# Bias and mask of a second attention enter its scores on TensorE instead of VectorE

## The chip, the cores and the metric

One Trainium2 chip, one of its cores. The metric is the device time of one execution of the whole kernel in microseconds, the median of three runs.

## What is computed

A two-layer decoder block over 128 sequences of 64 positions with 128 features, all in float32: causal attention, a gated cross layer, a mixture of experts, then a second layer with causal attention, cross-attention with a bias, and a second mixture of experts. The change is in the cross-attention of the second layer (16 heads of 8, `attn_bias` and `attention_mask` the same for all heads of a sequence):

```python
qh = (q @ Wq + bq).reshape(b, n, HEADS, DK).transpose(0, 2, 1, 3)
kh = (k @ Wk + bk).reshape(b, -1, HEADS, DK).transpose(0, 2, 1, 3)
vh = (v @ Wv + bv).reshape(b, -1, HEADS, DK).transpose(0, 2, 1, 3)
scores = jnp.einsum('bhnd,bhmd->bhnm', qh * scale, kh)
scores = scores + attn_bias[:, None, :, :] + attention_mask[:, None, :, :]
probs = jax.nn.softmax(scores, axis=-1)
ctx = jnp.einsum('bhnm,bhmd->bhnd', probs, vh)
```

## The kernel before

The 8192 rows (128 sequences x 64 positions) are cut into 64 tiles of 128 rows; a tile holds two whole sequences. The kernel runs in stages, one after the other over all tiles: the first layer's attention, a table of position products, a third stage (the first layer's gated cross layer and the attention of its expert block), the first experts, the fifth stage (from 2790 to about 3810 us), the second experts, a last sum.

The fifth stage combines the first experts' output into x4 (`combine5`, VectorE L1837 to L1842, from rows that GpSimd fetches at L2084), normalises it (L1537), runs the causal attention (called `a5[0]`, "the first attention"), a layer norm, the cross-attention (`a5[1]`, "the second attention"), another norm, and the logits of the router. It is one software pipeline. Each engine has a hand-written `period(i, j)` that lists its work for several tiles at once: in period i the causal attention is at tile i, the cross-attention's scores at tile i-2, its output at tile i-3, x4 at tile i+2. An engine executes its list strictly in this order; between engines there are counting semaphores, and `after(engine, signals...)` makes an engine wait for given counts. The loop over periods is unrolled four times.

TensorE's list of one period: weighted sum of the second attention (`weigh5`, L907); output projection of the first (L1054); transposition of x4 for tile i+2 (L1066, waits for `norms[0]`, that is, for VectorE's L1537); scores of the second attention for tile i-2 (`scores5`, L892); two transpositions (L1072, L1075); turning of the first attention's probabilities (`turn5`, L901); queries and keys of tile i+2 (L1084); router logits and keys (L1089, L1093); weighted sum of the first attention (L907); projection (L1054); values (L921); half of the turning of the second attention's probabilities; masks (L881) and scores (L892) of the first attention for tile i+1; the other half; then x5's transposition (L1115) and query (L1120).

`scores5` writes 128 rows x 16 heads x 64 keys into two PSUM banks of 512 columns, by four products of a 64x64 quarter of the array each, with the keys of the head pairs spread into a block-diagonal form (GpSimd's `spread5`, L1989, twice a period: b_k into `shared`, rope_k into `k_bd`). For the causal attention, a bf16 product of the identity with the mask starts the banks (`masks`, L881) and the scores are added to it. The second attention's scores start the banks themselves. GpSimd has added bias and mask of the tile once, 128x64, into `fm` (L2092). VectorE then adds `fm` to the scores, broadcast over 8 heads, one bank at a time (`bias_and_shift5`: add L1828, max L1831, subtract L1833), with the norm's L1537 between the two banks. For the first attention `shift5` (max L1551, subtract L1553) reads the PSUM bank directly. ScalarE takes the exponential (L1256) and copies turned probabilities (L1260). VectorE's list of a period goes on with `divide5` of the first attention (L1543, L1545), rope (L1559), the sum and norm statistics of tile i-3, `combine5` and statistics for tile i+3, and the shift of the first attention's scores for tile i+1; the next period begins with L1537 for x4.

Of the kernel before, what the change touches and what calls it, by code (L numbers as in the profile page):

```python
# [29 lines left out]
ALU = mybir.AluOpType  # L30
AX = mybir.AxisListType.X

P = 128
S = 64
# [6 lines left out]
NR = 2  # L41
V = 4
U = 2
# [57 lines left out]
def build(nc, T, out):  # L101
    B = T["x"].shape[0]
    NT = B * S // P
# [4 lines left out]
    with ExitStack() as ctx:  # L108
# [29 lines left out]
        scores_ps = ps("scores_ps", [P, U, NR, 512])  # L138
# [213 lines left out]
        def attention(a, tiles, shift_start, shift_per):  # L352

            return Attention(Signal(sc_ready[a], tiles), Signal(sub_ready[a], shift_start, shift_per), Signal(exp_ready[a], 2 * tiles, 2),
                             Signal(tr_ready[a], 2 * tiles, 2), Signal(tr_copied[a], 2 * tiles, 2), Signal(pv_ready[a], tiles),
                             Signal(ctx_ready[a], 2 * tiles, 2), Signal(ct_ready[a], tiles))
# [33 lines left out]
        norm_rstd = [again(m_rstd), again(f_rstd), again(r4_added)]  # L390
        rotated, rope_added, a_spread, b_spread = again(f_rotated), again(f_added, 2), again(m_spread), again(f_spread)
        fm_added, x5b_added = again(g_spread), again(xb_added)
        a5 = [attention(0, NT, 4 * NT, 4), attention(1, 2 * NT, 8 * NT, 6)]

        hop_dram = dram("hop_dram", [B * S, MH * S])
        xn_dram, r4_dram = dram("xn_dram", [B * S, D]), dram("r4_dram", [B * S, D])
# [327 lines left out]
        def _(pe):  # L724
# [152 lines left out]
            pe.wait_ge(s["hop_out0"], S + CREDIT)  # L877
            pe.wait_ge(s["hop_out1"], S + CREDIT)

            def masks(a, bank):  # L880
                pe.matmul(bank, ident16, causal16.unsqueeze(1).broadcast_to([P, 8, S]), start=True, stop=False,  # L881
                          skip_group_check=True)

            def scores5(at, a, q, keys, causal):
                if causal:
                    for g in range(NR):
                        masks(a, scores_ps[:, a, g, :])
                by_pair = keys.rearrange("p (h t) -> p h t", t=P)
                for g in range(NR):
                    rows = slice(64 * g, 64 * g + 64)  # L890
                    for b in range(NB):
                        last = pe.matmul(scores_ps[S * b:S * b + S, a, g, :], q[rows, S * b:S * b + S],  # L892
                                         by_pair[rows, :, S * b:S * b + S], start=not causal, stop=True,
                                         skip_group_check=True)
                last.then_inc(at.score.sem, 1)

# [30 lines left out]
            def period(i, j):  # L927
# [61 lines left out]
                    pe.matmul(desk_ps[:, 0:8], x_T[u], f_gate[:], start=True, stop=True, skip_group_check=True)\  # L989
                      .then_inc(f_logits.sem, 1)  # L990
                if live(i - 1):
                    after(pe, f_spread.of(i - 1), a3.copied.of(i - 2))
                    scores5(a3, 1, q_ring[:, 1 - u, :], k_ring[2 + 1 - u], True)
                if live(i + 1):
                    after(pe, m_copied.of(i + 1), m_v_ready.of(i + 1), gated.of(i + 7), block_done.of(i + 5) if j4 == 2 else gated.of(i + 7),
                          mixed.of(i, 5))
# [60 lines left out]
            def period(i, j):  # L1057
# [7 lines left out]
                    after(pe, norms[0].of(i + 2), rotated.of(i + 1))  # L1065
                    pe.transpose(heads_ps[:, 0:P], x4[(j + 2) % UN], ident).then_inc(x4_turned.sem, 1)  # L1066
                if live(i - 2):
                    after(pe, (zeroed, U + 1), b_q_copied.of(i - 2), b_spread.of(i - 2), a5[1].copied.of(i - 3))
                    scores5(a5[1], 1, b_q[u], k_ring[2 + u], False)
                if live(i - 4):  # L1070
                    after(pe, norms[2].of(i - 4), a_v_copied.of(i + 1), b_q_copied.of(i - 2), logits_copied.of(i - 5))
                    pe.transpose(desk_ps[:, 0:P], x6[u], ident).then_inc(x6_turned.sem, 1)  # L1072
# [33 lines left out]
                if live(i - 2):  # L1106
                    turn5(a5[1], 1, i - 2, 0)
                if live(i + 1):
                    after(pe, a_spread.of(i + 1), a5[0].copied.of(i))
                    scores5(a5[0], 0, q_ring[:, 1 - u, :], k_ring[1 - u], True)  # L1110
                if live(i - 2):
                    turn5(a5[1], 1, i - 2, 1)
                if live(i - 1):
# [310 lines left out]
        def _(dve):  # L1424
# [397 lines left out]
                dve.tensor_copy(got_w[u], weight[:, :, bass.ds(tile, 1)].rearrange("p k t -> p (k t)"))\  # L1822
                   .then_inc(s["weights_got"], 1)

            def bias_and_shift5(n, u, g):
                biased = probs[1][:, 512 * g:512 * g + 512].rearrange("p (h t) -> p h t", t=S)
                best = row_max[1][:, 8 * g:8 * g + 8]
                dve.tensor_tensor(biased, scores_ps[:, 1, g, :].rearrange("p (h t) -> p h t", t=S),  # L1828
                                  fm[u].unsqueeze(1).broadcast_to([P, 8, S]), ALU.add).then_inc(a5[1].shift.sem, 1)
                after(dve, a5[1].shift.of(n, 3 * g + 1))  # L1830
                dve.tensor_reduce(best, biased, AX, ALU.max).then_inc(a5[1].shift.sem, 1)  # L1831
                after(dve, a5[1].shift.of(n, 3 * g + 2))
                dve.tensor_tensor(biased, biased, best.unsqueeze(2).broadcast_to([P, 8, S]), ALU.subtract)\  # L1833
                   .then_inc(a5[1].shift.sem, 1)

            def combine5(n, u):
                dve.tensor_copy(got_w[u], weight[:, :, bass.ds(n, 1)].rearrange("p k t -> p (k t)")).then_inc(norms[0].sem, 1)  # L1837
                after(dve, norms[0].of(n, 1), (in_loaded[u], X4_LOADS + 8 * (n - u) + 16), (got_loaded[u], 16 * (n - u) + 32))
# [6 lines left out]
            def period(i, j):  # L1845
                u = j % U
                if live(i + 2):
                    apply5(norms[0], 0, u, x4[(j + 2) % UN], x4_raw[u], norm_rstd[0].of(i + 2), x4_turned.of(i - 2))
                if live(i - 4):
                    apply5(norms[2], 2, u, x6[u], b_sum[u], norm_rstd[2].of(i - 4), (x6_stored[u], 8 * (i - 4 - u) + 16), x6_turned.of(i - 6))  # L1850
                if live(i - 3):
                    divide5(a5[1], 1, i - 3)
                if live(i - 1):
                    after(dve, out_ready[0].of(i - 1))
                    dve.tensor_tensor(a_sum[1 - u], heads_of[0][:, 256:384], x4[(j - 1) % UN], ALU.add).then_inc(norms[1].sem, 1)
                    stats5(norms[1], 1, 1, i - 1, 1 - u, a_sum[1 - u])
                if live(i - 2):
                    after(dve, a5[1].score.of(i - 2), fm_added.of(i - 2))
                    bias_and_shift5(i - 2, u, 0)
                if live(i - 1):  # L1860
                    apply5(norms[1], 1, 1 - u, x5[1 - u], a_sum[1 - u], norm_rstd[1].of(i - 1), x5_turned.of(i - 3), x5b_added.of(i - 3))
                if live(i - 2):
                    bias_and_shift5(i - 2, u, 1)
                if live(i):
                    divide5(a5[0], 0, i)
                if live(i + 2):
                    after(dve, a_roped.of(i + 2), rope_added.of(i))
                    rope5(rotated, u)
                if live(i - 3):
                    after(dve, out_ready[1].of(i - 3), x5b_added.of(i - 3))  # L1870
                    dve.tensor_tensor(b_sum[1 - u], heads_of[1][:, 256:384], x5b[(j - 3) % UN], ALU.add).then_inc(norms[2].sem, 1)
                    stats5(norms[2], 1, 2, i - 3, 1 - u, b_sum[1 - u])
                if live(i + 3):
                    combine5(i + 3, 1 - u)
                    stats5(norms[0], 3, 0, i + 3, 1 - u, x4_raw[1 - u])
                if live(i + 1):
                    after(dve, a5[0].score.of(i + 1))
                    shift5(a5[0], 0, i + 1, 0)
                    shift5(a5[0], 0, i + 1, 1)
# [58 lines left out]
        def _(pool):  # L1938
# [149 lines left out]
            def period(i, j):  # L2088
                u = j % U
                if live(i - 1):  # L2090
                    after(pool, (c_loaded[1 - u], SIDE_LOADS + 24 * (i - 1 - (1 - u)) + 48), a5[1].shift.of(i - 3))
                    pool.tensor_tensor(fm[1 - u], fm_in[1 - u][:, 0:S], fm_in[1 - u][:, S:2 * S], ALU.add)\  # L2092
                        .then_inc(fm_added.sem, 1)
                    after(pool, norms[1].of(i - 1, norms[1].per - 1))
                    rstd5(norm_rstd[1], 1, 1 - u)
# [80 lines left out]
```

## Time and profile before

| | us |
|---|---|
| median of three runs | 4609.91 (4608.22 to 4623.54) |
| profiled execution | 4590.88 |
| its span, first to last instruction | 4588.8 |
| TensorE busy | 3012.8 (66%) |
| VectorE busy | 2698.5 (59%) |
| ScalarE busy | 1592.8 (35%) |
| GpSimd busy | 1899.0 (41%) |

The mean granted TensorE clock of the span is 0.779 of full speed. All times of instructions are from one profiled execution, in microseconds from the first instruction. Ends of TensorE's instructions are modelled. In groups and timelines a line reads: engine, line of the kernel, operation, output <- inputs, shapes, count, then busy time and mean duration, or start and duration; "idle" is the time in which the engine did nothing just before, with what ended it. A float32 product shows as two MATMUL records, a transposition as one.

### The profile page before, as it was taken

Reading aid. Unit: us, or ns where it says so; the run is one execution under the profiler, and the core shown is the slowest. Engines: PE = TensorE matmul, PEld = TensorE weight load, DVE = VectorE, ACT = ScalarE, POOL = GpSimd, SP = SyncE. Lnnn points to the kernel's source line nnn. Section 1 sums busy time; section 2 is a strip of 40 time slices with the busy share of each in tenths; the row PEclk is TensorE's granted clock in tenths of the full one; section 3 lists DMA queues with packets and bytes.
Section 4 is the critical chain, followed back from the end, with each engine's and each line's share of the span. In section 5 each row is a group of like instructions: output and inputs, shape, how many; then the busy total and the mean of one; then the engine's idle time right before and its main releaser. Section 6 shows DMA issues by size and latency. Waiting matters only on the chain.

```text
span 4588.8 us, 91966 instructions
## 1 busy us (share of the span) xinstructions
PE 3012.8 (66%) x27246; PEld 2049.9 (45%) x27249; DVE 2698.5 (59%) x7148; ACT 1592.8 (35%) x3994; POOL 1899.0 (41%) x2306
## 2 busy tenths in 40 slices
PE   4999998567666666666602887888888881056610
PEld 2666664344444444444401565555655561045510
DVE  2777775366666666666510115888888885034445
ACT  2666664233333333333201333455555450011100
POOL 4222220144444444444365004555656552721157
PEclk9999998766776776676656997888888885578965
DMA  2111113411111111111012221001010100211123
GB/s 52 40 39 39 39 39 107 158 32 30 30 35 31 30 35 31 30 30 30 18 61 69 74 71 34 25 24 27 25 27 24 24 22 26 78 51 55 55 75 85
DMA packets 282376, 207.13 MB, mean 45 GB/s; under 512 B 61730, under 2 KB 246455, under 8 KB 281904
## 3 DMA queue, kind: packets, MB, share of 16 engines
q1 hardware_dynamic: 262960, 164.88, 12.2%
q0 software_dynamic: 19200, 39.62, 3.1%
q8 instruction: 105, 1.72, 0.2%
q14 instruction: 111, 0.91, 0.1%
HBM read 114.99 MB, written 90.18 MB: 45 GB/s over the span
## 4 chain that ended last, share of the span: by engine, by line
PE 18%; issue 14%; DVE 13%; POOL 3%; SPq 1%; DVEq 1%; DMA 0%; ACT 0%; another core or an unknown queue 0%; POOLq 0%; ACTq 0%
PE scores_ps L1035 3%; PE scores_ps L892 3%; DVE row_max L1551 2%; DVE z L1842 2%; POOL rows L2039 1%; PE scores_ps L901 1%; PE heads_ps L1084 1%; PE desk_ps L1042 1%; PE heads_ps L1042 1%; PE scores_ps L1145 1%; PE turned_ps L907 1%; POOL shared L2136 1%; DVE probs L1828 1%; DVE norm_stat L1529 1%; PE scores_ps L1147 1%
## 5 line engine op out<-in xcount | busy, mean ns | idle before, releaser
L1985 POOL TENSOR_TENSOR norm_rstd<-norm_veps,minus_half 128x1 f32<-128x1 f32 x384 | 243.9, 635 | 467.2 <-DVE norm_veps L1533 467.0
L901 PE MATMUL scores_ps<-consts,probs 128*128 128x128 f32 x1536 | 302.2, 340 | 144.6 <-ACT probs L1256 143.9
L901 PEld LDWEIGHTS scores_ps<-consts,probs 128*128 128x128 f32 x1536 | 221.6, 174 | 234.7 <-ACT probs L1256 230.4
L2039 POOL DMA_INDIRECT rows<-e_in,slot_put x256 | 249.0, 973 | 164.0 <-issue 107.4
L1256 ACT ACTIVATE probs<-probs 128x512 f32<-128x512 f32 x384 | 241.7, 629 | 178.3 <-DVE probs L1553 166.2
L1260 ACT ACTIVATE turned<-scores_ps 128x512 f32<-128x512 f32 x384 | 225.0, 594 | 71.0 <-PE scores_ps L901 55.9
L1470 DVE TENSOR_REDUCE row_max<-scores_ps 128x8 f32<-128x512 f32 x256 | 175.0, 683 | 62.9 <-PE scores_ps L755 58.1
L1188 ACT ACTIVATE probs<-probs 128x512 f32<-128x512 f32 x256 | 161.3, 630 | 136.4 <-DVE probs L1472 133.9
L985 PE MATMUL scores_ps<-consts,probs 128*128 128x128 f32 x256 | 71.1, 433 | 184.4 <-DVE probs L1648 184.4
L1894 DVE COPY shared<-turned_ps 128x256 f32<-128x256 f32 x72 | 30.6, 425 | 264.8 <-issue 168.4
L1553 DVE TENSOR_TENSOR probs<-scores_ps,row_max 128x512 f32<-128x512 f32 x256 | 177.1, 692 | 8.9
L1472 DVE TENSOR_TENSOR probs<-scores_ps,row_max 128x512 f32<-128x512 f32 x256 | 177.1, 692 | 8.8
L1551 DVE TENSOR_REDUCE row_max<-scores_ps 128x8 f32<-128x512 f32 x256 | 174.8, 683 | 0.2 <-PE scores_ps L892 0.2
L2126 POOL TENSOR_TENSOR o_rstd<-o_veps,minus_half 128x2 f32<-128x2 f32 x72 | 49.9, 693 | 299.5 <-DVE o_veps L1914 289.7
L1559 DVE TENSOR_TENSOR rope_c<-heads_ps,consts 128x256 f32<-128x256 f32 x128 | 53.7, 420 | 201.9 <-PE heads_ps L966 195.6
L907 PE MATMUL turned_ps<-v_bd,turned 128*64 128x18 f32 x4096 | 158.4, 222 | 17.2 <-issue 17.0
L1192 ACT ACTIVATE turned<-scores_ps 128x512 f32<-128x512 f32 x256 | 144.7, 595 | 62.0 <-PE scores_ps L764 62.0
L764 PE MATMUL scores_ps<-consts,probs 128*128 128x128 f32 x1024 | 152.1, 281 | 15.2 <-ACT probs L1188 15.2
L907 PEld LDWEIGHTS turned_ps<-v_bd,turned 128*64 128x64 f32 x4096 | 148.0, 153 | 29.0 <-issue 21.3
L1137 PE MATMUL turned_ps<-consts,shared 128*128 128x128 f32 x144 | 32.1, 310 | 196.2 <-issue 196.2
L1977 POOL TENSOR_TENSOR shared<-k_raw,consts 128x1024 f32<-128x1024 f32 x32 | 60.7, 1896 | 241.2 <-issue 225.5
L2007 POOL TENSOR_TENSOR q_ring<-rope_c,rope_s 128x128 f32<-128x128 f32 x64 | 29.1, 455 | 312.4 <-DVE rope_s L1559 312.4
(338 smaller groups left out, 9019.0 us busy)
## 6 DMA issues: line engine op xcount, KB each, us to landing
hop_dram<-shared SPq DMA_DIRECT2D x64, 256.0 KB, 2.1
hop_in<-hop_dram SPq DMA_DIRECT2D x64, 256.0 KB
rows<-zero_rows SPq DMA_DIRECT2D x64, 144.0 KB
shared<-rows SPq DMA_DIRECT2D x72, 128.0 KB
moe<-shared SPq DMA_DIRECT2D x72, 128.0 KB, 1.9
rows<-zero_rows SPq DMA_DIRECT2D x64, 128.0 KB
c_in<-in_ctx SPq DMA_DIRECT2D x128, 64.0 KB
c_two<-in_ctx SPq DMA_DIRECT2D x128, 64.0 KB
```

What stands on the lines that cost most here:

```text
L764: last = pe.transpose(scores_ps[:, a, g, P * k:P * k + P], probs[a][:, P * hp:P * hp + P], ident)
L901: last = pe.transpose(scores_ps[:, a, g, P * k:P * k + P], probs[a][:, P * hp:P * hp + P], ident)
L907: last = pe.matmul(heads_of[a][S * b:S * b + S, 18 * hp:18 * hp + 18], turned[a][:, P * hp + S * b:P * hp + S * b + S], v[:, 36 * hp + 18 ...
L1188: act.activation(half, half, ACT.Exp, scale=SCALE).then_inc(exp_ready[a], 1)
L1256: act.activation(half, half, ACT.Exp, scale=scale).then_inc(at.exped.sem, 1)
L1260: act.activation(turned[a][:, 512 * g:512 * g + 512], scores_ps[:, a, g, :], ACT.Identity)\
L1470: dve.tensor_reduce(best, sc, AX, ALU.max).then_inc(sub_ready[a], 1)
L1472: dve.tensor_tensor(probs[a][:, 512 * g:512 * g + 512].rearrange("p (h t) -> p h t", t=S), sc, best.unsqueeze(2).broadcast_to([P, 8, S]), ...
L1551: dve.tensor_reduce(best, sc, AX, ALU.max).then_inc(at.shift.sem, 1)
L1553: dve.tensor_tensor(probs[a][:, 512 * g:512 * g + 512].rearrange("p (h t) -> p h t", t=S), sc, best.unsqueeze(2).broadcast_to([P, 8, S]), ...
L1985: pool.tensor_tensor(n_rstd[:, k, u, :], n_veps[:, k, u, :], minus_half[:, 0:1], ALU.pow).then_inc(sig.sem, 1)
L2039: pool.indirect_dma_start(out=rows, out_offset=bass.IndirectOffsetOnAxis(ap=slot_put[:, c, U * n + i:U * n + i + 1], axis=0), in_=put_rows ...
```

## The change

The two additions of `fm` on VectorE are taken out; the second attention now uses `shift5` as the first does, and its shift semaphore counts four steps per tile, not six. On TensorE a new helper `bias5` starts both banks of the second attention's scores with a float32 product of the identity and `fm`, broadcast over 8 heads (128 x 512 columns per bank); the scores are then added. TensorE now waits for `fm_added`, VectorE doesn't; GpSimd's next write of `fm` waits for the scores of its former tile instead of the shift. Bias products and causal masks are issued ahead of the wait for keys and queries, in the third stage too; the place of the scores in TensorE's order is the same.

```diff
-        a5 = [attention(0, NT, 4 * NT, 4), attention(1, 2 * NT, 8 * NT, 6)]
+        a5 = [attention(0, NT, 4 * NT, 4), attention(1, 2 * NT, 8 * NT, 4)]
...
+            def causal5(a):
+                for g in range(NR):
+                    pe.matmul(scores_ps[:, a, g, :], ident16, causal16.unsqueeze(1).broadcast_to([P, 8, S]),
+                              start=True, stop=False, skip_group_check=True)
+
+            def bias5(a, bias):
+                for g in range(NR):
+                    pe.matmul(scores_ps[:, a, g, :], ident, bias.unsqueeze(1).broadcast_to([P, 8, S]),
+                              start=True, stop=False, skip_group_check=True)
...
                 if live(i - 1):
-                    after(pe, f_spread.of(i - 1), a3.copied.of(i - 2))
-                    scores5(a3, 1, q_ring[:, 1 - u, :], k_ring[2 + 1 - u], True)
+                    after(pe, a3.copied.of(i - 2))
+                    causal5(1)
+                    after(pe, (zeroed, U + 1), f_spread.of(i - 1))
+                    scores5(a3, 1, q_ring[:, 1 - u, :], k_ring[2 + 1 - u])
...
                 if live(i - 2):
-                    after(pe, (zeroed, U + 1), b_q_copied.of(i - 2), b_spread.of(i - 2), a5[1].copied.of(i - 3))
-                    scores5(a5[1], 1, b_q[u], k_ring[2 + u], False)
+                    after(pe, a5[1].copied.of(i - 3), fm_added.of(i - 2))
+                    bias5(1, fm[u])
+                    after(pe, (zeroed, U + 1), b_q_copied.of(i - 2), b_spread.of(i - 2))
+                    scores5(a5[1], 1, b_q[u], k_ring[2 + u])
...
                 if live(i + 1):
-                    after(pe, a_spread.of(i + 1), a5[0].copied.of(i))
-                    scores5(a5[0], 0, q_ring[:, 1 - u, :], k_ring[1 - u], True)
+                    after(pe, a5[0].copied.of(i))
+                    causal5(0)
+                    after(pe, (zeroed, U + 1), a_spread.of(i + 1))
+                    scores5(a5[0], 0, q_ring[:, 1 - u, :], k_ring[1 - u])
...
-            def bias_and_shift5(n, u, g):
...
                 if live(i - 2):
-                    after(dve, a5[1].score.of(i - 2), fm_added.of(i - 2))
-                    bias_and_shift5(i - 2, u, 0)
+                    after(dve, a5[1].score.of(i - 2))
+                    shift5(a5[1], 1, i - 2, 0)
...
                 if live(i - 2):
-                    bias_and_shift5(i - 2, u, 1)
+                    shift5(a5[1], 1, i - 2, 1)
...
-                    after(pool, (c_loaded[1 - u], SIDE_LOADS + 24 * (i - 1 - (1 - u)) + 48), a5[1].shift.of(i - 3))
+                    after(pool, (c_loaded[1 - u], SIDE_LOADS + 24 * (i - 1 - (1 - u)) + 48), a5[1].score.of(i - 3))
                     pool.tensor_tensor(fm[1 - u], fm_in[1 - u][:, 0:S], fm_in[1 - u][:, S:2 * S], ALU.add)\
```

## Rows read from the trace of the kernel before

**Rows 1.** Busy time by window; columns: window, length, engines, clock, DMA.
```profile
core 0: us, PE busy (x) PEld busy (x) DVE busy (x) ACT busy (x) POOL busy (x), PEclk, DMA share, GB/s
2880.00:3750.00 870.00, 738.63 (x7726) 514.90 (x7726) 736.91 (x1846) 444.01 (x1176) 507.63 (x667) 0.83 0.10 25
```

**Rows 2.** Waits of 2880 to 3750 us: us in total, times, longest.
```profile
PE heads_ps L1066 <- DVE g_diag L1537: 92.5, 56, 2.9
...
DVE probs L1828 <- PE scores_ps L892: 42.1, 55, 0.8
...
DVE recip L1543 <- PE turned_ps L907: 36.5, 32, 1.3
```

**Rows 3.** Timeline, first tile: start, duration, engine, line, operation [idle before].
```profile
3096.92 0.48 PE L1066 MATMUL heads_ps<-consts,g_diag 128*128 128x128 f32 x1 [2.26 <-DVE g_diag L1537]
...
3102.32 1.11 PE L907 MATMUL turned_ps<-v_bd,turned 128*64 128x18 f32 x32
...
3103.74 1.90 POOL L1989 TENSOR_TENSOR shared<-hop_in,consts 128x1024 f32<-128x1024 f32 x1 [0.78 <-ACT hop_in L1373]
3103.75 0.25 DVE L1543 RECIPROCAL recip<-turned_ps 128x16 f32<-128x16 f32 x1
...
3105.42 1.09 PE L892 MATMUL scores_ps<-k_bd,q_ring 64*64 64x512 f32 x8
...
3106.78 0.35 DVE L1842 SCALAR_TENSOR_TENSOR z<-got,got_w,h_mid 128x128 f32<-128x128 f32 x1
...
3106.98 1.91 POOL L1989 TENSOR_TENSOR k_bd<-rope_k,consts 128x1024 f32<-128x1024 f32 x1
```

**Rows 4.** Timeline, second tile.
```profile
3110.90 0.48 PE L1066 MATMUL heads_ps<-consts,g_diag 128*128 128x128 f32 x1 [0.70 <-DVE g_diag L1537]
...
3111.30 1.98 PE L892 MATMUL scores_ps<-shared,hop_in 64*64 64x512 f32 x8
...
3117.79 1.11 PE L907 MATMUL turned_ps<-v_bd,turned 128*64 128x18 f32 x32
...
3118.66 1.90 POOL L1989 TENSOR_TENSOR shared<-hop_in,consts 128x1024 f32<-128x1024 f32 x1 [1.73 <-ACT hop_in L1373]
...
3118.95 0.26 DVE L1543 RECIPROCAL recip<-turned_ps 128x16 f32<-128x16 f32 x1 [1.15 <-PE turned_ps L907]
...
3121.90 1.89 POOL L1989 TENSOR_TENSOR k_bd<-rope_k,consts 128x1024 f32<-128x1024 f32 x1
3121.90 2.04 DVE L1842 SCALAR_TENSOR_TENSOR z<-got,got_w,h_mid 128x128 f32<-128x128 f32 x1
```

**Rows 5.** Timeline, beginning of the third tile.
```profile
3127.74 0.47 PE L1066 MATMUL heads_ps<-consts,g_diag 128*128 128x128 f32 x1 [2.37 <-DVE g_diag L1537]
```

**Rows 6.** Busy time by window (columns as in Rows 1), cut where the granted clock changes.
```profile
3096.67:3100.08 3.41, 3.16 (x13) 1.33 (x14) 2.43 (x9) 0.94 (x3) 0.69 (x2) 0.50 0.20 58
...
3110.32:3117.15 6.83, 6.25 (x28) 4.42 (x29) 5.72 (x16) 2.81 (x7) 3.15 (x5) 0.50 0.18 49
```

**Rows 7.** Groups by line and shape, 2880 to 3750 us: busy, mean ns | idle before.
```profile
L1553 DVE TENSOR_TENSOR probs<-scores_ps,row_max 128x512 f32<-128x512 f32 x112 | 77.5, 692 | 3.9
L1828 DVE TENSOR_TENSOR probs<-scores_ps,fm 128x512 f32<-128x512 f32 x112 | 77.0, 687 | 42.1 <-PE scores_ps L892 42.1
...
L1551 DVE TENSOR_REDUCE row_max<-scores_ps 128x8 f32<-128x512 f32 x112 | 76.4, 682 | 0.0
```

**Rows 8.** Timeline of the first experts' stage (2600 to 2612 us), TensorE.
```profile
2600.70 3.69 PE L1035 MATMUL scores_ps<-e_T,e_w 128*128 128x512 f32 x8 [1.47 <-DVE e_T L1798]
2604.23 3.73 PE L1042 MATMUL heads_ps<-e_w,shared 128*128 128x128 f32 x32
```

**Rows 9.** Instructions of L2092, 3090 to 3112 us: duration in ns, first and last start.
```profile
L2092 POOL TENSOR_TENSOR fm<-fm_in x2: 315/316/317, 3094.6 to 3109.4; 128x64 f32<-128x64 f32 x2
```

**Rows 10.** Masks of L881 in the whole kernel, and the idle time before them (us, times).
```profile
L881 PE MATMUL scores_ps<-consts x256: 379/587/634, 930.0 to 3764.2; 128*128 128x512 bf16 x128
...
  POOL shared L1989: 4.8, 4
```

More of the change, by code:

```diff
@@ L878, in _, with scores5 @@
             pe.wait_ge(s["hop_out1"], S + CREDIT)
[L880 to L887, printed above, removed]
+            def causal5(a):
[6 more added lines that the diff above has]
+                              start=True, stop=False, skip_group_check=True)
+            def scores5(at, a, q, keys):
                 by_pair = keys.rearrange("p (h t) -> p h t", t=P)
@@ L892, in scores5 @@
                         last = pe.matmul(scores_ps[S * b:S * b + S, a, g, :], q[rows, S * b:S * b + S],
-                                         by_pair[rows, :, S * b:S * b + S], start=not causal, stop=True,
+                                         by_pair[rows, :, S * b:S * b + S], start=False, stop=True,
                                          skip_group_check=True)
@@ L1823, in get_weights @@
                    .then_inc(s["weights_got"], 1)
-            def bias_and_shift5(n, u, g):
[L1826 to L1834, printed above, removed]
             def combine5(n, u):
```

## The prediction

> **What bounds the kernel now.** I first asked how much of the kernel the edit can reach. The lines that it takes off VectorE (L1828, L1831, L1833) run only in the fifth stage. The window table gives that stage's steady part: 870 us in which TensorE (738.6 us) and VectorE (736.9 us) are busy for the same 85% [rows 1]. Neither is full, so shares don't decide; the order does. TensorE waits at L1066, which runs once a tile, 56 times in it [rows 2], so a tile takes 870 / 56 = 15.54 us.
>
> The waits of that window come next [rows 2]. TensorE stands longest at L1066, the transposition of x4, until VectorE's L1537 has written x4: 92.5 us in 56 tiles. VectorE waits for the second attention's scores (42.1 us) and, 32 times, for the products of L907 (36.5 us). So the work passes to and fro. I read it off the timeline of two neighbouring tiles.
> - TensorE's leg: from L1066 (held by L1537) through the scores of the second attention (L892), two transpositions, the turning of the first attention's probabilities (L901), L1084, L1093 and the first attention's weighted sum (L907). At its end VectorE can divide (L1543). In the first tile it runs from 3096.92 to 3102.32 + 1.11 = 3103.43: 6.51 us [rows 3]. In the second from 3110.90 to 3117.79 + 1.11 = 3118.90: 8.00 us [rows 4].
> - VectorE's leg: from L1543 through rope, sums, the far part (L1842), the shift of the first attention's scores, to L1537 and the next L1066. First tile 3103.75 to 3110.90: 7.15 us; second 3118.95 to 3127.74: 8.79 us [rows 3 to 5].
>
> Two things make the tiles unequal. (a) The granted clock: 0.50 for 3.41 us around the first tile's L1066 and for 6.83 us around the second's, 1.00 between (1.2 and 2.4 GHz) [rows 6]. Each drop follows a wait at L1066. (b) L1842 takes 0.35 us in one and 2.04 us in the other: there it starts together with GpSimd's spread L1989 (both 3121.90, until 3123.8), in the first it starts 0.20 us before it [rows 3, 4]. The sums are 13.98 and 16.84 us; their mean, 15.41, is close to the measured 15.54.
>
> **Part 1, off VectorE.** Two additions of 128x512 per tile go: 2 x 0.69 = 1.38 us [rows 7]. The max and the subtraction stay; they now read PSUM, as L1551 and L1553 do for 682 and 692 ns, no more than L1828's 687 [rows 7]. Where do the 1.38 us lie? Between the scores' landing and L1543, beside TensorE's L901 to L907. In the first tile L1543 starts at 3103.75 without having waited, so VectorE's own work held it; L907 ended at 3103.43 and would have let it start at 3103.48: the saving is worth 0.27 us. In the second tile VectorE already waits 1.15 us before L1543: nothing more [rows 3, 4]. What is late next is TensorE itself.
>
> **Part 2, onto TensorE.** Two full products per tile, 128x128 by 512 columns in f32. The nearest rows are those of L1035, same shape and type at full clock: eight records, that is four products, from 2600.70 to the next line at 2604.23: 0.88 us each [rows 8]. So 1.76 us at full clock. At half clock twice that, 3.5 us, as L892's eight records take 1.09 us at full clock and 1.98 at half [rows 3, 4]. They stand in TensorE's order behind L1066 and ahead of L892, inside the leg. TensorE's idle time lies before L1066, where they can't start; nothing hides them. Behind them wait the scores and all that follows.
>
> A slow stretch of given length only halves the work done in it. If it keeps its 3.4 or 6.8 us, the leg grows by exactly the 1.76 us of full-clock work: 6.51 + 1.76 = 8.27 us, or 8.00 + 1.76 = 9.76 us. VectorE follows 0.05 us after (3118.90 to 3118.95).
>
> **Part 3, the waits.** The products wait for `fm_added` of the same tile. GpSimd makes it at 3094.6 and 3109.4, just before L1066, and for the next tile round; so it lies some 16 us ahead of its use [rows 9]. Cost nothing; the cover is that round. GpSimd's own wait moves from VectorE's shift to TensorE's score, which comes earlier. Splitting the wait lists adds a few wait instructions; now all of the way from L1066's start to L892's is 0.40 us (3110.90 to 3111.30 [rows 4]), half of it L1066's own work. Behind running products it is covered. If not: up to 0.2 us a tile. In the third stage and for the first attention here the bf16 masks are only moved ahead of the wait for GpSimd's spread. TensorE stood there for that spread 4 times, 4.8 us in all [rows 10]. I take 0, bounds -4.8 and +13 us (0.2 x 64).
>
> **Part 4, the far part L1842.** Whether it is blocked depends on when L1543 comes against GpSimd's first spread. First tile: 3103.75 and 3103.74, free; second: 3118.95 and 3118.66, blocked [rows 3, 4]. In the second the slow stretch reached over L1084, which delays L907 but not the other path as much. After the change a slow stretch of 6.8 us beginning 0.6 us before L1066 ends 6.2 us after it, while L1084 starts only about 0.4 + 3.5 + 2.0 + 0.5 + 1.2 = 7.6 us after it. So L901 to L907 run as in the first tile, and L1543 comes 0.27 us earlier there than now. I take L1842 as free: VectorE's leg 7.15 us.
>
> **The sum.** A tile takes 8.27 + 0.05 + 7.15 = 15.47 us with a short slow stretch and 9.76 + 0.05 + 7.15 = 16.96 us with a long one. Their mean is 16.2 us, since both occur now in turn. Against 15.54: +0.68 us x 64 tiles = +43 us. On the profiled run's own 4590.9 us that is 4634; that run is 0.4% under the median of the runs shown, 4609.9, so I forecast 4653 us. The two ends of this case are -4 us (all short: 4606) and +91 us (all long: 4701).
>
> The Trainium skill (TensorE: Matmul & The Clock Gate, "What's actually happening") says that throttled is the default state and activity releases it. By that rule dense products right behind L1066 should shorten the slow stretches, which is the second rival below. The trace agrees that drops follow idleness.
>
> **The rivals.**
> 1. Other side: the clock stays up. The drop follows idle time ahead of L1066, and dense work might fill enough of each tile to prevent it. Then TensorE's leg is 6.51 - 1.55 (half of the 3.1 us that were slow) + 1.76 = 6.72 us, the tile 13.92 us, -1.62 x 64 = -104 us: 4506. It decides once more than about half of the tiles have no slow stretch. For it: much denser work per tile. Against: the 2.37 us wait at L1066 [rows 5] belongs to VectorE's leg, which doesn't change. 0.13, mostly in part, around 4560 to 4590.
> 2. Slow stretches all become short: 4606, no change. For it: the work behind L1066 is denser now. 0.15.
> 3. L1842 is blocked in every tile, because TensorE's leg now always ends last: 8.27 + 0.05 + 8.79 = 17.11 us, +1.57 x 64 = +100 us: 4710. For it: all tiles where VectorE waited for L907 are of the blocked kind. 0.12. The Trainium skill (SBUF — State Buffer, "Who interferes with whom") says that a VectorE instruction with two SBUF inputs and a GpSimd one that reads SBUF exclude each other, the later waiting for the whole of the other. The start times of L1842 agree.
> 4. VectorE is the bound after all and the whole 1.38 us comes back: -88 us, 4522. Against: 1.15 us of waiting before L1543 in every second tile. 0.05.
> The forecast has 0.55.
>
> **Range and chances.** The range reaches into rival 1's partial form and to rival 3: 4560 to 4715. Within 0.3% (14 us, about what a measurement of this kernel can tell from no change) lies rival 2: 0.15. Faster: rivals 1 and 4, 0.18. Slower: 0.67.
>
> **What would show it.** In the profile after: about 3.5 us of new product time per tile mostly at half clock, directly behind L1066; VectorE's wait at its first max of the second attention well over 0.77 us (some 2 to 4 us); VectorE's busy time in the stage down by 77 us in 56 tiles; the wait at L1066 still there. The sum is wrong if L1842's median stays at 2 us (rival 3), if the granted clock of the stage rises clearly above 0.83 with tiles under 15 us (rival 1), or if VectorE does not wait for the scores longer (rival 4).

## The result and the profile after

The changed kernel takes 4657.99 us (median of four runs, 4655.49 to 4661.47), the kernel before 4615.23 us (four runs, 4608.22 to 4623.54) beside it. The ratio is 1.0092 with a 95% interval of 1.0071 to 1.0114: slower by 43 us. The profiled execution has a span of 4658.2 us, against 4588.8.

The window table of the changed kernel over the same 870 us shows where to look; columns as in [rows 1]:

```profile
2880.00:3750.00 870.00, 721.84 (x7233) 456.98 (x7231) 640.12 (x1580) 397.91 (x1069) 463.61 (x611) 0.90 0.09 23
```

VectorE is less busy (640.1 us for 736.9) and the granted clock higher (0.90 for 0.83), yet fewer instructions pass (VectorE 1580 for 1846). The waits of this window, to be held against [rows 2], say how many tiles passed:

```profile
DVE row_max L1560 <- PE scores_ps L895: 148.2, 50, 3.2
...
PE heads_ps L1071 <- DVE g_diag L1546: 112.9, 51, 2.4
...
DVE recip L1552 <- PE turned_ps L910: 36.6, 51, 0.7
```

51 tiles in 870 us instead of 56: 17.06 us each. VectorE now waits 2.9 us a tile for the second attention's scores (148.2 / 51) and at every division for L910, which was L907. L1071, L895, L904, L910, L1100, L1840 and L1987 are the old L1066, L892, L901, L907, L1093, L1842 and L1989; L1546 and L1552 the old L1537 and L1543. One tile of the timeline, which answers to [rows 3 to 5]:

```profile
3114.28 0.47 PE L1071 MATMUL heads_ps<-consts,g_diag 128*128 128x128 f32 x1 [2.27 <-DVE g_diag L1546]
3114.55 3.28 PE L887 MATMUL scores_ps<-fm,consts 128*128 128x512 f32 x4
3117.76 1.09 PE L895 MATMUL scores_ps<-shared,hop_in 64*64 64x512 f32 x8
...
3121.07 0.47 PE L1100 MATMUL desk_ps<-c_T,c_w 128*128 128x128 f32 x2
3121.47 1.11 PE L910 MATMUL turned_ps<-v_bd,turned 128*64 128x18 f32 x32
...
3121.72 0.18 ACT L1378 ACTIVATE logits<-desk_ps 128x16 f32 x1 [0.69 <-PE desk_ps L1100]
...
3122.25 1.90 POOL L1987 TENSOR_TENSOR shared<-hop_in,consts 128x1024 f32<-128x1024 f32 x1 [1.13 <-ACT hop_in L1382]
...
3122.63 0.26 DVE L1552 RECIPROCAL recip<-turned_ps 128x16 f32<-128x16 f32 x1 [0.71 <-PE turned_ps L910]
...
3125.51 2.04 DVE L1840 SCALAR_TENSOR_TENSOR z<-got,got_w,h_mid 128x128 f32<-128x128 f32 x1
3125.51 1.89 POOL L1987 TENSOR_TENSOR k_bd<-rope_k,consts 128x1024 f32<-128x1024 f32 x1
...
3131.31 0.47 PE L1071 MATMUL heads_ps<-consts,g_diag 128*128 128x128 f32 x1 [1.90 <-DVE g_diag L1546]
```

TensorE's leg runs from 3114.28 to 3121.47 + 1.11 = 3122.58: 8.30 us. VectorE's runs from 3122.63 to 3131.31: 8.68 us, because L1840 and GpSimd's second spread start together and L1840 takes 2.04 us. The clock, cut at its steps, is low once in this tile and for 3.41 us (compare [rows 6]):

```profile
3113.89:3117.30 3.41, 3.02 (x5) 1.28 (x5) 1.88 (x9) 0.91 (x2) 0.69 (x2) 0.51 0.20 57
3117.30:3130.95 13.65, 11.25 (x139) 7.78 (x137) 10.65 (x24) 6.87 (x19) 8.43 (x10) 1.00 0.06 15
```

It is so in nearly every tile: counted after 2880 us, 55 low stretches of 3.4 us and none of 6.8; before it was 23 and 32. And L1840 is blocked nearly always. The group of its 64 instructions gives least, median and most in ns:

```profile
L1840 DVE SCALAR_TENSOR_TENSOR z<-got,got_w,h_mid x64: 352/2041/2110, 2787.7 to 3825.1; 128x128 f32<-128x128 f32 x64
```

The median of the same line before was 1172 ns; counted one by one, it took over 1 us in 32 of 64 tiles before and in 56 of 64 now. A median that stays at 2 us is one of the prediction's own signs that its sum is wrong (rival 3).

### The profile page after: what moved, and what is told of

Same layout as the page of the kernel before. It is cut to its first block, busy times and chain, and to the rows that moved or that the text cites. A ratio compares the mean times of both kernels' runs of the same rounds, so it can differ in the third digit from the quotient of the medians.

```text
span 4658.2 us, 92118 instructions
## 1 busy us (share of the span) xinstructions
PE 3082.7 (66%) x27502; PEld 2045.7 (44%) x27505; DVE 2644.7 (57%) x7020; ACT 1587.1 (34%) x3994; POOL 1898.4 (41%) x2306
## 4 chain that ended last, share of the span: by engine, by line
PE 22%; issue 12%; DVE 12%; POOL 4%; DVEq 1%; DMA 0%; ACT 0%; POOLq 0%; ACTq 0%; SPq 0%
PE scores_ps L887 4%; PE scores_ps L1040 3%; DVE z L1840 3%; POOL rows L2037 2%; DVE row_max L1560 2%; PE turned_ps L910 2%; POOL shared L2134 2%; PE scores_ps L895 2%; PE heads_ps L1091 1%; PE scores_ps L904 1%; PE scores_ps L1154 1%; PE heads_ps L1047 1%; PE desk_ps L1047 1%; DVE norm_stat L1538 1%; PE scores_ps L1156 1%
## 5 line engine op out<-in xcount | busy, mean ns | idle before, releaser
L1560 DVE TENSOR_REDUCE row_max<-scores_ps 128x8 f32<-128x512 f32 x384 | 262.6, 684 | 185.7 <-PE scores_ps L895 185.7
L904 PE MATMUL scores_ps<-consts,probs 128*128 128x128 f32 x1536 | 266.0, 309 | 138.9 <-ACT probs L1265 138.1
L904 PEld LDWEIGHTS scores_ps<-consts,probs 128*128 128x128 f32 x1536 | 185.4, 154 | 228.8 <-ACT probs L1265 223.7
L1562 DVE TENSOR_TENSOR probs<-scores_ps,row_max 128x512 f32<-128x512 f32 x384 | 265.5, 691 | 13.3
L1479 DVE TENSOR_REDUCE row_max<-scores_ps 128x8 f32<-128x512 f32 x256 | 174.8, 683 | 62.9 <-PE scores_ps L755 58.1
L887 PE MATMUL scores_ps<-fm,consts 128*128 128x512 f32 x256 | 201.7, 940 | 0.0
L988 PE MATMUL scores_ps<-consts,probs 128*128 128x128 f32 x256 | 71.1, 433 | 185.4 <-DVE probs L1657 185.4
L1481 DVE TENSOR_TENSOR probs<-scores_ps,row_max 128x512 f32<-128x512 f32 x256 | 176.9, 691 | 8.8
L910 PE MATMUL turned_ps<-v_bd,turned 128*64 128x18 f32 x4096 | 159.8, 223 | 16.4 <-issue 16.0
L764 PE MATMUL scores_ps<-consts,probs 128*128 128x128 f32 x1024 | 152.8, 282 | 15.1 <-ACT probs L1197 15.1
L910 PEld LDWEIGHTS turned_ps<-v_bd,turned 128*64 128x64 f32 x4096 | 149.4, 154 | 28.1 <-issue 20.0
```

The costliest lines, as they stand in the source:

```text
L887: pe.matmul(scores_ps[:, a, g, :], ident, bias.unsqueeze(1).broadcast_to([P, 8, S]), start=True, stop=False, skip_group_check=True)
L904: last = pe.transpose(scores_ps[:, a, g, P * k:P * k + P], probs[a][:, P * hp:P * hp + P], ident)
L910: last = pe.matmul(heads_of[a][S * b:S * b + S, 18 * hp:18 * hp + 18], turned[a][:, P * hp + S * b:P * hp + S * b + S], v[:, 36 * hp + 18 ...
L1479: dve.tensor_reduce(best, sc, AX, ALU.max).then_inc(sub_ready[a], 1)
L1481: dve.tensor_tensor(probs[a][:, 512 * g:512 * g + 512].rearrange("p (h t) -> p h t", t=S), sc, best.unsqueeze(2).broadcast_to([P, 8, S]), ...
L1560: dve.tensor_reduce(best, sc, AX, ALU.max).then_inc(at.shift.sem, 1)
```

## The experiments

The runs are compared by their ratio to the kernel before on the same chip. For the stage I give the mean tile after the eighth, its two legs (from the start of L1066 to that of L1543, and on to the next L1066), in how many of 64 tiles the far part (L1842) took over 1 us, and how many low stretches of 3.4, of 6.8 and of 10.2 us lay after 2880 us. Tiles, legs and stretches come from the one execution that was profiled, medians and ratios from all. For e2, e5, e7 and e10 the profiled execution is the longest of its kernel, for e2 by 19 us over the median. e2 leaves bias and mask out of the scores, e3 enters them twice.

| kernel | median us | ratio (95%) | tile us | legs us | far part blocked | low stretches |
|---|---|---|---|---|---|---|
| before, first profile | 4615 | | 15.56 | 7.53 + 8.03 | 32 | 23, 32, 0 |
| e1, before again | 4611 | 0.9985 (0.9968 to 1.0002) | 16.09 | 7.74 + 8.35 | 42 | 22, 26, 7 |
| the changed kernel | 4658 | 1.0092 (1.0071 to 1.0114) | 17.05 | 8.37 + 8.69 | 56 | 55, 0, 0 |
| e2, additions off only | 4598 | 0.9973 (0.9954 to 0.9992) | 16.21 | 7.50 + 8.71 | 57 | 13, 43, 0 |
| e3, products on only | 4851 | 1.0512 (1.0483 to 1.0542) | 20.06 | 11.41 + 8.65 | 54 | 6, 37, 13 |
| e5, before, far part first | 4496 | 0.9724 (0.9703 to 0.9745) | 14.07 | 6.87 + 7.20 | 0 | 38, 8, 0 |
| e4, after, far part first | 4487 | 0.9722 (0.9696 to 0.9749) | 14.10 | 7.08 + 7.01 | 0 | 7, 0, 0 |
| e9, e4 with products twice | 4651 | 1.0090 (1.0056 to 1.0124) | 16.42 | 9.42 + 7.00 | 0 | 29, 0, 0 |
| e6, after, products early | 4563 | 0.9869 (0.9847 to 0.9890) | 15.24 | 5.81 + 9.44 | 58 | 24, 0, 0 |
| e7, e6 and e4 | 4438 | 0.9599 (0.9578 to 0.9619) | 13.26 | 5.09 + 8.17 | 0 | 4, 0, 0 |
| e10, e5 with idle products early | 4476 | 0.9703 (0.9670 to 0.9736) | 13.68 | 6.36 + 7.31 | 0 | 1, 0, 0 |
| e8, masks moved only | 4619 | 0.9993 (0.9983 to 1.0002) | 16.09 | 7.67 + 8.42 | 43 | 19, 32, 4 |

### e1: how steady is the kernel before?

No edit.

> The kernel before, unchanged, profiled a second time. Its profiled run (4590.9 us) lies under its other runs (4608 to 4624 us), while the changed kernel's profiled run (4660) agrees with its own. Theory 1 (the tiles of the fifth stage fall into kinds of 14.0 and 16.8 us, and how many of each differs from run to run): another profile shows a different share of 16.8 us tiles, a mean tile of 15.5 to 16.1 us in the stage, and the total follows it. Theory 2 (the difference lies elsewhere): the mean tile is 15.54 us again and another stage differs. Ratio 1.000.

The total is the same, the profile is not. The transpositions of x4, before (first line, [rows 5] is one of them) and in the changed kernel, mark the stage:

```profile
L1066 PE MATMUL heads_ps<-consts,g_diag x64: 328/476/476, 2794.2 to 3781.2; 128*128 128x128 f32 x64
```

```profile
L1071 PE MATMUL heads_ps<-consts,g_diag x64: 327/473/476, 2790.2 to 3829.2; 128*128 128x128 f32 x64
```

From first to last it is 987 us here, 956 us in the profile that I predicted from (2790.8 to 3747.0), 1039 us in the changed kernel. Theory 1 holds for this pair of profiles: the mean tile is 16.09 us, the far part is blocked in 42 tiles, not 32, and the total is 18 us longer (span 4607.1). What lies behind the last L1066 differs too, by 16 us the other way (826 and 842 us), so the stages don't account for it alone. The changed kernel's gap to this second profile is 51.1 us in span, and the stage grew by 52 us.

### e2 and e3: the two halves of the change

```diff
# e2: the changed kernel, no bias products
-                    after(pe, a5[1].copied.of(i - 3), fm_added.of(i - 2))
-                    bias5(1, fm[u])
-                    after(pe, (zeroed, U + 1), b_q_copied.of(i - 2), b_spread.of(i - 2))
-                    scores5(a5[1], 1, b_q[u], k_ring[2 + u])
+                    after(pe, (zeroed, U + 1), b_q_copied.of(i - 2), b_spread.of(i - 2), a5[1].copied.of(i - 3))
+                    scores5(a5[1], 1, b_q[u], k_ring[2 + u], True)     # start=True
# e3: the kernel before, products added, VectorE's additions kept
+                    after(pe, a5[1].copied.of(i - 3), fm_added.of(i - 2))
+                    for g in range(NR):
+                        pe.matmul(scores_ps[:, 1, g, :], ident, fm[u].unsqueeze(1).broadcast_to([P, 8, S]),
+                                  start=True, stop=False, skip_group_check=True)
```

> The changed kernel without the two bias products on TensorE: bias and mask are left out of the scores altogether, the second attention's scores start their banks themselves, VectorE does max and subtraction alone. It shows what the removal of VectorE's additions is worth by itself. Legs theory (TensorE's leg and VectorE's leg alternate): the 1.38 us removed lie beside TensorE's leg, worth 0 to 0.27 us a tile, so 0 to -17 us: 4600 to 4615 against 4615. Rival (VectorE is the bound): -1.38 x 64 = -88 us, 4527.

> The kernel before with the two bias products added ahead of the second attention's scores, VectorE's additions kept (bias and mask so enter twice): the addition to TensorE by itself. Legs theory: products cost as in the change, and after the scores VectorE's own 4.45 us now end later than TensorE's 3.8 us, so a tile takes 17.07 + 0.7 = 17.7 us: about 4700. Rival (the additions on VectorE cost nothing in either arrangement): 17.07 us as in the changed kernel, 4658. Rival (products hidden): 4615.

e2: 0.9973, a median 14 us under that of before; the legs theory's 0 to 17 us, not the rival's 88 us. Taking 1.38 us a tile off VectorE is worth next to nothing while TensorE's leg ends last. But it has a side effect that I had not named: the far part is now blocked in 57 of 64 tiles (42 in e1), and VectorE's leg grows by 0.36 us while TensorE's shrinks by 0.24. In its profile VectorE, without the additions, nearly always waits for the weighted sum, and then it nearly always meets the spread.

e3: 4851 us, 150 more than expected. The tile is 20.06 us where I had 17.7. Its timeline shows why:

```profile
3133.64 0.69 DVE L1832 TENSOR_TENSOR probs<-scores_ps,fm 128x512 f32<-128x512 f32 x1 [3.92 <-PE scores_ps L892]
...
3137.04 1.90 POOL L1993 TENSOR_TENSOR shared<-hop_in,consts 128x1024 f32<-128x1024 f32 x1 [0.47 <-ACT hop_in L1377]
...
3137.39 2.10 DVE L1837 TENSOR_TENSOR probs<-probs,row_max 128x512 f32<-128x512 f32 x1
```

With the additions kept, the second subtraction (L1837, both inputs in SBUF) meets GpSimd's first spread and takes 2.10 us instead of 0.69. That is 1.4 of the 2.4 us missed. In the changed kernel the subtraction (L1562) reads its scores from PSUM; its mean is 691 ns in the same window. The low stretches are long here, 50 of 56 of them 6.8 or 10.2 us, which would be the rest; that part is only argued. So the products need the removal of the additions: alone they cost 5.1%, together 0.9%.

### e4 and e5: the far part ahead of GpSimd's spread

```diff
-                    after(pool, rope_added.of(i + 2))
+                    after(pool, rope_added.of(i + 2), norms[0].of(i + 3, 3))
                     spread5(k_ring[u], rope_k[u], "head16").then_inc(a_spread.sem, 1)
```

e4 has this edit in the changed kernel, e5 in the kernel before. GpSimd's second spread then waits until VectorE has written z.

> The changed kernel; GpSimd's spread of rope_k (into k_bd) waits until VectorE has finished the far part (L1840), so the two never start together. Theory 1 (in the changed kernel L1840 is blocked by that spread in every tile, 2.04 instead of 0.35 us, and this lies on VectorE's leg): L1840 falls to 0.35 us, the tile from 17.07 to about 15.4 us, 64 x -1.6 = -100 us: 4560. Theory 2 (the tile is held at 17.07 us by the clock's low stretches; a shorter leg is given back by a longer low stretch): L1840 falls, the low stretch grows from 3.4 to 6.8 us, the tile stays near 17 us: 4650.

> The kernel before with the one edit of e4: GpSimd's second spread waits for VectorE's far part (L1842). Together with before, after and e4 it makes a square. Theory 1 (legs): L1842 free in every tile, VectorE's leg 7.15 us; the low clock stretches stay, since nothing dense was added, so tiles are 6.5 or 8.0 + 0.05 + 7.15 = 13.7 to 15.2 us, mean 14.4: against the 16.1 us of the second profile of before about -100 us, 4510, a little slower than e4's 4486. Theory 2 (the change is itself a gain of e4): without it the tile stays at 15.4 us or more, 4570.

Both of the first theories hold, and the gain is larger than I expected. The far part of e4:

```profile
L1840 DVE SCALAR_TENSOR_TENSOR z<-got,got_w,h_mid x64: 351/352/428, 2785.1 to 3654.8; 128x128 f32<-128x128 f32 x64
```

Never blocked. The waits of e4 over 720 us, and its window:

```profile
DVE row_max L1560 <- PE scores_ps L895: 84.9, 51, 3.1
```

```profile
2880.00:3600.00 720.00, 658.02 (x7253) 434.86 (x7251) 557.03 (x1586) 399.74 (x1075) 465.88 (x613) 0.99 0.11 28
```

51 tiles in 720 us, 14.1 us each, with the clock at 0.99. VectorE's leg fell from 8.69 to 7.01 us, by the 1.69 us that the far part lost; TensorE's fell from 8.37 to 7.08 us, and the low stretches all but vanished (55 to 7). That the second fact makes the first fits an estimate: 48 stretches fewer, 1.7 us of work lost in each, over 55 tiles are 1.5 us a tile. TensorE's wait at L1071 fell too, from 2.2 to 0.5 us a tile. e5 over the same stretch:

```profile
2880.00:3600.00 720.00, 630.96 (x7074) 446.94 (x7074) 642.37 (x1691) 404.56 (x1074) 486.30 (x615) 0.89 0.11 28
```

The square is plain. Without the collision of the far part the change is worth nothing: 0.9724 before, 0.9722 after. With the collision it costs 0.9%. In e5 the clock is 0.89 with 46 low stretches, in e4 0.99 with 7, and TensorE's leg is only 0.21 us longer for 1.76 us more of full-clock work. The clock can pay for it: by the same estimate e5 loses 92 us to its low stretches and e4 12 us, which is 1.5 us a tile.

### e9: the price of the products where no low stretch is left

```diff
                     bias5(1, fm[u])
+                    bias5(1, fm[u])
```

> e4 with the two bias products issued twice (the second pair writes the same banks anew): another 1.76 us of full-clock work at the same place. Between e5 and e4 the first pair cost nothing in the total. Theory 1 (the first pair was paid for by the low clock stretches it removed; hardly any are left in e4): the second pair costs its full 1.76 us a tile, tile 14.1 to 15.9 us, +64 x 1.76 = +113 us: 4600. Theory 2 (products there are hidden beside VectorE's work): as e4, 4486.

Theory 1: 4651 us against e4's 4487, so the second pair is not hidden. It costs more than its full-clock price: the tile grows by 2.32 us, TensorE's leg by 2.34. The low stretches are back (29), in which the work takes double; 22 more of them than in e4 are 0.7 us a tile by the estimate above, and 0.6 us are to be explained. The place costs full price once the clock has nothing to give. Why the stretches come back isn't shown. TensorE has more work than in e4 and waits no longer at L1071. Over 720 us it is 0.51 us a tile in both, e4 first, then e9:

```profile
PE heads_ps L1071 <- DVE g_diag L1546: 26.0, 51, 1.5
```

```profile
PE heads_ps L1071 <- DVE g_diag L1547: 22.6, 44, 0.7
```

### e6, e7 and e10: the same products in TensorE's idle time

```diff
# e6, and with e4's edit e7: ahead of the wait for x4
+                if live(i - 2):
+                    after(pe, a5[1].copied.of(i - 3), fm_added.of(i - 2))
+                    bias5(1, fm[u])
                 if live(i + 2):
                     after(pe, norms[0].of(i + 2), rotated.of(i + 1))
```

e10 is e5 with the same two products in that place and start=True in the scores, which overwrite them; the additions stay on VectorE.

> The changed kernel with the two bias products ahead of TensorE's wait for x4 (L1071) instead of behind it, in the idle time of about 2.3 us there. Theory 1 (the products' cost is their place on TensorE's leg): the leg loses them, 1.76 us at full clock and the low stretch in part: 5 to 6.5 us; with L1840 still blocked a tile takes 13.8 to 15.3 us: 4470 to 4560. Theory 2 (only the blocked L1840 matters): 17 us as in the changed kernel, 4650.

> e6 and e4 together. Theory 1: both gains add, legs of 5.0 + 0.05 + 7.15 = 12.2 us if the clock stays up; VectorE's own work of some 11 us a tile and its waits then hold it at 12.2 to 13.2 us: 4611 - 61 x 3.4 = about 4400 (4370 to 4440). Theory 2 (the products ahead of the wait are of use only against the clock): as e4, 4486.

> e5 (additions on VectorE kept) with the same two products as idle work ahead of the wait for x4, their result overwritten by the scores. Theory 1 (early products only lift the clock; e7's further gain is the 1.38 us off VectorE, which is late once TensorE's leg is short): legs 5.7 + 8.2 = 13.9 us against e5's 14.07 and e7's 13.26: about 4490 (4475 to 4510). Theory 2 (the clock alone made e7): as e7, 4437.

e6: 4563 us, 3 us above the range. TensorE's leg falls from 8.37 to 5.81 us, so the products' cost was indeed their place. VectorE's leg grows from 8.69 to 9.44 us. The timeline has the far part blocked, and now for 2.4 us, and in the same tile L1836, a copy of 128x2, takes 0.97 us beside GpSimd's work (0.17 us in the changed kernel's tile):

```profile
3116.76 1.90 POOL L1988 TENSOR_TENSOR shared<-hop_in,consts 128x1024 f32<-128x1024 f32 x1
3118.12 0.97 DVE L1836 COPY got_w<-weight 128x2 f32 x1
...
3119.66 2.43 DVE L1841 SCALAR_TENSOR_TENSOR z<-got,got_w,h_mid 128x128 f32<-128x128 f32 x1
3120.05 1.89 POOL L1988 TENSOR_TENSOR k_bd<-rope_k,consts 128x1024 f32<-128x1024 f32 x1
```

e7 is the fastest kernel here: 4438 us, at the upper end of its range, 4.0% under before and by the ratios 4.9% under the changed kernel. TensorE's wait for x4, the largest wait of [rows 2], is gone; over 720 us:

```profile
DVE recip L1553 <- PE turned_ps L910: 37.6, 54, 0.7
DVE row_max L1561 <- PE scores_ps L895: 34.9, 46, 2.7
PE heads_ps L1074 <- DVE g_diag L1547: 0.3, 1, 0.3
```

The products aren't free there either. They now run past the moment at which VectorE has written x4, and the transposition waits for their end:

```profile
3122.56 1.88 PE L887 MATMUL scores_ps<-fm,consts 128*128 128x512 f32 x4
3122.95 0.34 DVE L1547 TENSOR_SCALAR g_diag<-z,norm_mv,norm_rstd 128x128 f32<-128x128 f32 x1
...
3124.28 0.27 PE L1074 MATMUL heads_ps<-consts,g_diag 128*128 128x128 f32 x1
```

x4 was there at 3123.29, and L1074 starts 0.99 us later. After the eighth tile this gap is 1.00 us on average, against 0.06 us in e4. It is most of the 1.16 us by which the second leg of e7 (8.17 us) exceeds that of e4 (7.01 us).

e10: 4476 us, as expected, though by legs of 6.36 + 7.31 us and not 5.7 + 8.2. Its ratio can't be told from that of e5 (0.9703 and 0.9724, the intervals overlap); in the profiles the low stretches fall from 46 to 1, and from the first to the last transposition of x4 it is 850 us for 872. e7 is another 1.0% faster by the ratios, and that comes with the additions off VectorE. There, with TensorE's leg at 5.1 us, the change does what it is for. Part of it is that the second attention's subtractions read PSUM: in e10, where they read SBUF, 58 of 120 took over 0.9 us.

### e8: the masks ahead of the wait

```diff
-                    after(pe, f_spread.of(i - 1), a3.copied.of(i - 2))
-                    scores5(a3, 1, q_ring[:, 1 - u, :], k_ring[2 + 1 - u], True)
+                    after(pe, a3.copied.of(i - 2))
+                    causal5(1)
+                    after(pe, (zeroed, U + 1), f_spread.of(i - 1))
+                    scores5(a3, 1, q_ring[:, 1 - u, :], k_ring[2 + 1 - u], True)
```

> The kernel before with only the causal masks moved ahead of the wait for GpSimd's spread, in the third stage and for the first attention of the fifth. My steps: 0, bounds -5 and +13 us: 4606 to 4624. Rival (the added waits cost TensorE's queue in the third stage): its window from 850 to 2790 us grows.

0.9993 (0.9983 to 1.0002): nothing, as priced. The third stage didn't grow either: the first L1066 comes at 2791.2 us here, at 2790.8 and 2794.2 us in the two profiles of the kernel before.

## Why the prediction was right, and where it wasn't

- **The view of the stage.** Two legs, to and fro, and neither engine full: right. It carried over to all kernels but e7, where the second leg ends with TensorE's own products.
- **Part 1.** At most 0.27 us of VectorE's 1.38 us: right in size (e2). It priced the subtraction by its duration alone, 0.69 us from PSUM as from SBUF, and left out what it does to GpSimd; see part 4.
- **Part 2.** The products on TensorE's leg, unhidden: right. The leg was forecast at 8.27 us with a short low stretch; it measured 8.30 us in the tile shown and 8.37 us on average, to L1552's start. The price of 1.76 us at full clock held nearly: in the changed kernel the products take 3.21 us (3114.55 to 3117.76), of which 2.75 lie in the low stretch, so 1.84 us of full-clock work. The low stretch, as assumed, did not grow for it.
- **The clock.** I had kept the mix of short and long low stretches. All became short, as in rival 2, and the stage's clock rose from 0.83 to 0.90. The Trainium skill (TensorE: Matmul & The Clock Gate, "What's actually happening") has activity releasing the throttle; the trace agrees here, and e4 beside e5 agrees. e9 beside e4 does not show it: more work, the same wait, and 29 low stretches for 7. The mean of 8.27 and 9.76 us was a mis-sized term: with the 0.05 us it is 9.07 us to L1552's start, and 8.37 was measured, 0.7 us less.
- **Part 4 failed.** I took the far part as free and VectorE's leg as 7.15 us; it is blocked nearly always and the leg is 8.69 us, so the tile 17.05 us: rival 3's mechanism, forecast at 17.11. The failed step is the carrying over of one row. In the first tile of [rows 3] L1543 and GpSimd's first spread started together, and I moved L1543 0.27 us ahead of it. In the changed kernel L1552 comes 0.38 us after the first spread, in the tile shown, and so the far part no longer comes ahead of the second one. The first spread had been late in that row, and no other profile has this lateness. ScalarE's L1369, which waits for L1093, started at 3103.21, 0.82 us after the end that the records give to L1093 (3102.39); in the changed kernel the same step is L1100's end at 3121.54 to L1378 at 3121.72, 0.18 us. The trace also keeps when the semaphores rise: L1093's rose at 3103.04, 0.65 us after that end. In this one profile it rose 0.6 to 0.8 us late in 24 of 60 tiles after 2880 us, in the eleven others in none (0.02 us at most), and nearly all free tiles of this profile are among the 24. What delayed it is open.

The second profile of the kernel before (e1) has free tiles for another reason, and this one the change removes:

```profile
3127.03 0.69 DVE L1833 TENSOR_TENSOR probs<-probs,row_max 128x512 f32<-128x512 f32 x1
3127.16 2.32 POOL L1989 TENSOR_TENSOR shared<-hop_in,consts 128x1024 f32<-128x1024 f32 x1 [0.31 <-ACT hop_in L1373]
...
3130.58 0.35 DVE L1842 SCALAR_TENSOR_TENSOR z<-got,got_w,h_mid 128x128 f32<-128x128 f32 x1
...
3130.97 1.89 POOL L1989 TENSOR_TENSOR k_bd<-rope_k,consts 128x1024 f32<-128x1024 f32 x1
```

Here VectorE's second subtraction, both inputs in SBUF, holds up GpSimd: the first spread takes 2.32 us, not 1.90, the second one comes later for it, and the far part is done before. It is so in 12 of the 15 free tiles after the eighth. In the changed kernel the subtraction reads PSUM, no first spread takes over 1.90 us, and one tile of 56 is free.

- **The base.** I counted from one profile with a tile of 15.54 us. A second one has 16.09. The kernel before falls now into one mix of tiles, now into another, and its runs spread over 15 us before any change (over 35 us in the 18 runs beside e1). I also set my mean of 16.2 us against the measured 15.54 and not against 15.41, the mean of the same two tiles; that took 8 us off the forecast.

The forecast of 4653 us came out within 5 us of 4658, and this is partly luck: the tile grew by 1.5 us against the profile that I used, not by 0.68. Against e1 it grew by 0.96 us, which by 64 is 61 us; the stages of the two profiles differ by 52, and 43 were measured. The missed collision (+1.5 us a tile) is partly offset by the clock (-0.7) and by the base (-0.5). The leg and the range stand on the steps, the last digits don't, and the direction only in part: against e1, 0.63 us of the growth is TensorE's leg, as forecast, and 0.33 us VectorE's, and without the collision the same products cost nothing (e4 beside e5). Rival 1's mechanism is real too and needed the collision out of the way: in e4 nearly all tiles run without a low stretch, at 14.10 us where it had 13.92.

## What to carry to other kernels

Work moved to another engine must be put into that engine's idle time in its order of issue, not beside the place where its result is used: ahead of the wait for x4 instead of behind it, the same two products made the kernel 2.2% faster with the collision (e6 against the changed kernel) and 1.2% without it (e7 against e4). The idle time must also be long enough: in e7 it is 1 us too short. Look in the trace for an instruction whose duration has two values (0.35 and 2.04 us here), find what starts with it on another engine, and order the two with a wait; that one wait was worth 2.8%, far more than the change. Before an operand moves between SBUF and PSUM, ask which other engine its reads had been holding up. And take more than one profile of a kernel whose tiles alternate before a prediction of a per cent is made from it.

## What the runs showed of the hardware

- A VectorE instruction with both inputs in SBUF and a GpSimd instruction that reads SBUF hold each other up: the far part (0.35 us alone) takes 2.04 us beside the spread, the subtraction 2.10 instead of 0.69, and the spread 2.32 instead of 1.90 us when the subtraction is already running (e1). With one input in PSUM the subtraction took 0.69 us in all of the changed kernel's window. The Trainium skill (SBUF — State Buffer, "Who interferes with whom") states this rule and the trace agrees.
- The start times in the records don't tell who wins. In the changed kernel's blocked tiles the spread's record starts between 0.03 us before and 0.07 us after the far part's, in e6 up to 0.39 us after it, and the far part is the one that waits each time: it ends 0.15 us after the spread in all of them.
- Two inputs in SBUF aren't the only case: in e6 a copy of 128x2 with one input took 0.97 instead of 0.17 us beside GpSimd's work.
- Dense products can cost next to nothing in time: 1.76 us of full-clock work a tile lengthened TensorE's leg by 0.21 us (e5 to e4), while the low stretches fell from 46 to 7. Another 1.76 us cost 2.34 us (e4 to e9), and the low stretches rose to 29.
